# Routing, expert projections and row softmax in one block: routing chunk by chunk, output constants prepared inside

## The reference, cut to what matters

```python
x = x + xattn_ref(layernorm(x), ctx, ctx, ...)      # 32 x 512 x 512, recurrence with gates, 8 heads of 64
h = layernorm(x)                                    # then 16 experts of width 64
def ffn(x, Wg, Wq, bq, Wkv, bkv, Wo, bo, ln_g, ln_b):
    h = transpose(x, (1, 0, 2))                     # 512 tokens, each with 32 candidate rows
    probs = softmax(h @ Wg)                         # over the 16 experts
    idx = sort(top_k(transpose(probs, (0, 2, 1)), cap=2))   # each expert takes 2 of a token's 32 rows
    hg = rows of h at idx
    q = hg @ Wq + bq;  k, v = split(hg @ Wkv + bkv)
    att = (q . k) * 64 ** -0.5                      # 2 x 2 per token and expert
    p = softmax(att, axis=1)                        # over all 512 tokens
    ao = (p @ v) @ Wo + bo
    y = h + scatter_add(ao at idx)
    return transpose(layernorm(y) * ln_g + ln_b)
x = x + ffn(layernorm(x), ...)
```

## Time and profile before

| what | value |
|---|---|
| median of 3 runs | 1986.8 us (1984.19 to 1990.59) |
| the profiled execution | 1991.78 us, span of the core 1990.0 us |
| granted TensorE clock, mean of the span | 0.943 |
| PE busy | 1680.2 us (84%) |
| DVE busy | 1386.0 us (70%) |
| ACT busy | 1087.6 us (55%) |
| POOL busy | 1221.4 us (61%) |

### The profile page before, as it was taken

The page is one execution under the profiler, slowest core; times in us unless marked ns, Lnnn a source line. Parts: engine busy times, 40 slices in busy tenths (PEclk is TensorE's granted clock), DMA queues, the critical chain, the costliest instruction groups (busy, mean ns, idle before and its releaser), DMA issues. The chain is left out here.

```text
span 1990.0 us, 58854 instructions
## 1 busy us (share of the span) xinstructions
PE 1680.2 (84%) x22734; PEld 1281.8 (64%) x22893; DVE 1386.0 (70%) x2931; ACT 1087.6 (55%) x2531; POOL 1221.4 (61%) x1218
## 2 busy tenths in 40 slices
PE   4898888988899888998989861599996799989894
PEld 3677777777777777777777751599995344444442
DVE  2577776777777777777777779233345298999998
ACT  3676776777767777676777640122221545454541
POOL 1566667676676666766767760477673375666664
PEclk9999999999999999999999985699998899999998
DMA  6132222222322222222231010645443257777686
GB/s 198 50 98 86 92 98 82 87 93 97 98 82 87 92 97 98 82 93 89 95 97 61 34 42 0 252 139 139 137 139 101 53 129 170 168 169 171 153 181 154
DMA packets 106597, 218.03 MB, mean 110 GB/s; under 512 B 13008, under 2 KB 14416, under 8 KB 105552
## 3 DMA queue, kind: packets, MB, share of 16 engines
q1 hardware_dynamic: 96080, 180.68, 31.8%
q0 software_dynamic: 10240, 33.56, 5.8%
HBM read 147.08 MB, written 67.11 MB: 108 GB/s over the span
## 5 line engine op out<-in xcount | busy, mean ns | idle before, releaser
L318 POOL TENSOR_TENSOR rec_hn<-rec_hn,rec_out_w 128x512 f32<-128x512 f32 x128 | 199.3, 1557 | 212.9 <-DVE rec_hn L739 212.9
L1320 POOL TENSOR_TENSOR out_x_half<-out_x_half,out_ln_b 128x512 f32<-128x512 f32 x128 | 163.7, 1310 | 154.0 <-DVE out_z_half L1490 154.0
L1424 PE MATMUL out_z_ps<-out_ao,out_hot 32*128 32x512 f32 x2048 | 234.6, 606 | 16.0 <-ACT out_ao L1352 11.5
L296 POOL TENSOR_TENSOR rec_hrs<-rec_harg,rec_minus_half 128x8 f32<-128x8 f32 x128 | 213.0, 1664 | 10.0
L1112 ACT ACTIVATE exp_rows_t<-exp_t_ps 128x512 f32<-128x512 f32 x128 | 69.5, 594 | 244.6 <-PE exp_t_ps L1080 240.0
L1424 PEld LDWEIGHTS out_z_ps<-out_ao,out_hot 32*128 32x128 f32 x2048 | 106.2, 189 | 141.8 <-issue 113.4
L1352 ACT ACTIVATE out_ao<-out_o_ps,sigma_rows 128x512 f32<-128x512 f32 x128 | 88.0, 687 | 193.7 <-PE out_o_ps L1412 193.7
L705 DVE TENSOR_TENSOR rec_c<-rec_s_ps,rec_d 128x512 f32<-128x512 f32 x256 | 164.9, 686 | 38.2 <-PE rec_s_ps L426 35.2
L536 ACT ACTIVATE rec_d<-rec_l_ps 128x512 f32<-128x512 f32 x256 | 151.7, 593 | 62.6 <-PE rec_l_ps L450 61.8
L1092 PE MATMUL exp_q_ps<-exp_wqkv,exp_rows_t 128*128 128x192 f32 x1024 | 178.4, 328 | 0.0
L1092 PEld LDWEIGHTS exp_q_ps<-exp_wqkv,exp_rows_t 128*128 128x128 f32 x1024 | 167.4, 192 | 0.0
(11 more groups left out here) (215 smaller groups left out, 4349.5 us busy)
## 6 DMA issues: line engine op xcount, KB each, us to landing
rec_x_ring<-in_x SPq DMA_DIRECT2D x128, 256.0 KB, 3.0
rec_ctx_ring<-in_ctx SPq DMA_DIRECT2D x128, 256.0 KB, 3.0
x_scratch<-rec_x_ring SPq DMA_DIRECT2D x128, 256.0 KB, 2.0
out_x_half<-x_scratch SPq DMA_DIRECT2D x128, 256.0 KB, 5.5
out<-out_x_half SPq DMA_DIRECT2D x128, 256.0 KB, 3.8
exp_wqkv<-in_wqkv SPq DMA_DIRECT2D x4, 1536.0 KB, 15.3
exp_x_rows<-x_scratch,rowid POOLq DMA_INDIRECT x128
out_wo<-in_wo SPq DMA_DIRECT2D x1, 2048.0 KB, 7.7
```

The lines of the kernel that those rows point to most:

```text
L296: nc.gpsimd.tensor_tensor(hrs[:, G % 2], harg[:, G % 2], mhalf[:], ALU.pow).then_inc(hrs_done, 1)
L318: nc.gpsimd.tensor_tensor(h, h, w8[:], ALU.mult).then_inc(hw_done, 1)
L1320: nc.gpsimd.tensor_tensor(xt[H % XR][:, q, :], xt[H % XR][:, q, :], lb[:], ALU.add).then_inc(xb_done, 1)
L1424: mm = nc.tensor.matmul(z_ps[r][:], hot[B % 2][g, hp, m * P:(m + 1) * P], ao[B % 2][g, hp, :], start=(hp == 0), stop=(hp == HP - 1))
```

## The change

Routing, experts and softmax become one block (`expert_stage`), so three blocks remain.

- The units run chunk outer: `c, h = divmod(m, NE)`. Only chunk 0 is routed before the units; chunk c + 1 is routed by DVE in 14 parts, one behind each unit of chunk c. `rowid_done` holds POOL's gather of a chunk until its indices are there.
- All 16 experts are centred within the first chunk: PE makes the means of experts 0 to 5 before the first unit and one more in each of the units 0 to 9, in two PSUM tiles; ACT copies them to SBUF (`copy_means`), and DVE subtracts the copy.
- The tables for the scatter come between units 46 and 53, by 4 matmuls each in place of 16. DVE sums the products unit by unit.
- The weights of experts 8 to 15 are loaded after the gather of unit 1 has landed; `Wo`, the bias and the vectors are loaded during units 16 to 32. The bias split, `cols` and the one-hot matrix of the first output step (`hot_first`) are made in units 48 to 62.
- In the output block the loads, the split and the first one-hot matrix are gone.

```diff
-def routing_tables(nc, scope, z, keep, tables, gather, consts):
-def expert_attention(nc, scope, z, x1_dram, wqkv, bqkv, tables, gather, vall, att):
-def softmax_over_rows(nc, scope, z, att, tables):
+def expert_stage(nc, scope, z, keep, x1_dram, wqkv, bqkv, wo_in, vecs, consts, tables, gather, prepared, vall, att):
+    UNITS, RING, EARLY = NE * NC, 6, 6
+    @block.sync
+        weights(0)
+        sp.dma_start(iotab[:], consts[26, :, 0:NI]).then_inc(const_in, 16)
+        sp.dma_start(ident[:], consts[0]).then_inc(const_in, 16)
+        sp.dma_start(tokid[:], consts[25]).then_inc(const_in, 16)
+        weights(1)
+        sp.dma_start(bias[:], bqkv).then_inc(b_in, 16)
+        sp.wait_ge(rows_in[1], 32)
+        weights(2)
+        weights(3)
+        sp.wait_ge(transposed, NE)
+        sp.dma_start(bo[:], vecs[0]).then_inc(bo_in, 16)
...
+    @block.gpsimd
+        def fetch(m):
+            c, h = divmod(m, NE)
+            if h == 0:
+                pool.wait_ge(rowid_done, c + 1)
...
+    @block.tensor
+        for h in range(EARLY):
+            weight_means(h)
+        pe.wait_ge(const_in, 48)
+        for m in range(UNITS + 1):
+            if m < UNITS:
+                transposes(m)
+            if m + EARLY < NE:
+                weight_means(m + EARLY)
+            if m == 46:
+                rows_of(m_ps[0], idx).then_inc(ip_full, 1)
+            if m == 50:
+                pe.wait_ge(sel_done, 1)
+                rows_of(m_ps[1], ssel).then_inc(sg_full, 1)
+            if m == 52:
+                pe.wait_ge(ip_read, 1)
...
+            if m > 0:
+                projections(m - 1)
...
+    @block.scalar
+        router_exp(0)
+        for h in range(EARLY):
+            copy_means(h)
+        for m in range(UNITS):
+            evict(m)
+            if m + EARLY < NE:
+                copy_means(m + EARLY)
+            if h == 2 and c + 1 < NC:
+                router_exp(c + 1)
+            if 53 <= m < 61:
+                distance(m - 53)
+            if m in (61, 62):
+                mark(m - 61)
...
+    @block.vector
+        for part_no in range(10):
+            route(0, part_no)
+        centre(0)
+        centre(1)
+        for part_no in range(10, 14):
+            route(0, part_no)
+        dve.wait_ge(b_in, 16)
+        for m in range(UNITS):
+            if m + 2 < NE:
+                centre(m + 2)
+            read(m)
+            if m:
+                logits(m - 1)
+            if c + 1 < NC:
+                route(c + 1, h)
...
+            if m == 50:
+                link(vec.tensor_reduce(colv[:], four[:], AX.X, ALU.add))
+                vec.tensor_scalar(colv[:], colv[:], base, None, ALU.add).then_inc(ip_read, 1)
...
 def output_stage
-        sp.dma_start(bo[:], vecs[0]).then_inc(bo_in, 16)
-        sp.dma_start(wo[:], wo_in).then_inc(w_in, 16)
-        sp.dma_start(lg[:], vecs[1]).then_inc(vec_in, 16)
-        sp.dma_start(lb[:], vecs[2]).then_inc(vec_in, 16)
...
-        pool.wait_ge(vec_in, 32)
-        act.wait_ge(dve_set, 1)
...
         spread(0)
-        for m in range(2):
-            for hp in range(4 * m, 4 * m + 4):
-                distance(0, hp)
-                evict(0, hp)
-            mark(0, m)
+        for hp in range(HP):
+            evict(0, hp)
```

More of the change, by code:

```diff
@@ L1004, in sem @@
         return scope.enter_context(nc.semaphore("exp_" + name))
+    iotab = sb("iotab", [P, NI])
+    peak = sb("peak", [P, NB])
+    total = sb("total", [P, NB])
+    eq = sb("eq", [P, NE, NB])
+    left = sb("left", [P, NE, NB])
+    m1 = sb("m1", [P, NE])
+    first = sb("first", [P, NE])
+    second = sb("second", [P, NE])
+    idx = sb("idx", [P, NC, NE, 2])
+    ssel = sb("sigma_sel", [P, NC, NE, 2])
+    var = sb("variance", [P, NC, NB])
+    each = sb("each_four", [P, 4 * P])
+    four = sb("four", [P, P, 4])
     w = sb("wqkv", [P, NE, KC, W3])
@@ L1094, in projections, with rows_of @@
             mm.then_inc(q_full, 1)
-        weight_means(0)
+        def rows_of(ps, table):
+            flat = table[:].rearrange("p c h i -> p (c h i)")
+            to = ps[:].rearrange("p (c b k) -> p b c k", c=NC, b=4)
+            for b in range(4):
+                mm = nc.tensor.matmul(to[:, b], each[:, P * b:P * b + P], flat, start=(b == 0), stop=(b == 3))
+            return mm
+        for h in range(EARLY):
+            weight_means(h)
+        pe.wait_ge(const_in, 48)
         for m in range(UNITS + 1):
@@ new lines, in _ @@
+            if m == 47:
+                vec.reciprocal(ssel[:].rearrange("p c h i -> p (c h i)"), rsel[:].rearrange("p c h i -> p (c h i)")
+                               ).then_inc(sel_done, 1)
+            if m == 48:
+                vec.tensor_copy(cols[:, 0:P], tokid[:]).then_inc(cols_done, 1)
+                vec.tensor_scalar(cols[:, P:2 * P], tokid[:], float(P), None, ALU.add).then_inc(cols_done, 1)
+                vec.memset(ones[:], 1.0)
+            if m == 49:
+                dve.wait_ge(ip_full, 1)
+                own(m_ps[0])
@@ L1524, in program @@
-        with ExitStack() as routed:
-            keep = (sb(routed, "probs_all", [P, z.NC, NE, NB]), sb(routed, "rstd_all", [P, z.NC, NB]))
-            with ExitStack() as scope:
-                recurrence_stage(nc, scope, NB, (x, ctx, consts, gate_w, gate_b, out_w, wg), x1_dram, keep)
-            with ExitStack() as scope:
-                routing_tables(nc, scope, z, keep, tables, gather, consts)
-        vall = sb(kept, "v_all", [P, z.NC, NE, 2, z.DH])
-        att = sb(kept, "att", [P, z.NC, NE * 4])
@@ L1532, in program, with sb @@
-        with ExitStack() as scope:
-            expert_attention(nc, scope, z, x1_dram, wqkv, bqkv, tables, gather, vall, att)
+        def sb(name, shape, dt=F32):
+            return kept.enter_context(nc.sbuf_tensor(name, shape, dt))
+        probs = sb("probs_all", [P, z.NC, NE, NB])
+        keep = (probs, sb("rstd_all", [P, z.NC, NB]))
+        with ExitStack() as scope:
+            recurrence_stage(nc, scope, NB, (x, ctx, consts, gate_w, gate_b, out_w, wg), x1_dram, keep)
+        tables = tuple(sb(name, [P, P]) for name in ("colv", "sigma_rows", "eps_var", "tokid", "ident2"))
@@ L1536, in program @@
         with ExitStack() as scope:
[L1537 removed]
+            output_stage(nc, scope, z, x1_dram, out, prepared, tables, vall, att)
 def shape_constants():
```

456 lines of the change are left out of this document (205 added, 251 removed).

## The result

| what | before | after |
|---|---|---|
| median of the runs of this comparison | 1988.69 us (1984.19 to 1994.59, 4 runs) | 1908.25 us (1905.3 to 1913.83, 4 runs) |
| span of the profiled execution | 1990.0 us | 1908.6 us |
| granted TensorE clock, mean of the span | 0.943 | 0.965 |
| DVE busy | 1386.0 us | 1406.2 us (74%) |
| POOL busy | 1221.4 us | 1233.8 us (65%) |

The ratio of after to before is 0.9597, with a 95% interval of 0.9561 to 0.9633: 4.0% faster. The forecast was 1907.6 us, counted from a median before of 1986.8; in this comparison the median before is 1988.69. As a gain, 79.2 us were forecast; 80.4 were measured on the medians and 81.4 in the spans.

A forecast was written before the change was run, and what follows sets the result against it. PE bounds the units and the output has DVE and PE busy, but some 145 us are at no engine's limit. Terms 67.8 - 0.4 + 1.9 + 8.0 + 1.9 = 79.2 us take the median from 1986.8 to 1907.6, range 1899 to 1917.

The forecast's parts named there:

- 1. Routing of chunk 0: Start of the new block: DVE's routing ahead of the first gather takes 13.2 us, row numbers at 1202.1 against 1233.
- 2. First gather and first units: From row numbers to first read: first transposes at 1207.1, first read at 1214.8 against 1282.6; gain so far 67.8 us.
- 3. The loop: First to last read of the units: 238.0 us against 237.6, PE work saved is eaten by waits; loss 0.4.
- 4 to 6. Softmax, output start, first evictions: After the last read: shorter way into softmax 1.9, POOL's earlier product 8.0, ACT's marks gone before first scatter 1.9 us gained.
- POOL and DVE in series: Units' loop: descriptor writing too excludes DVE's two-operand work, so their times add; 17 us more, 1925, or 1934; chance 0.17.
- gathers over 1.0: Units' loop: POOL's gathers taking over 1.0 us were listed among the signs that the prediction is wrong.
- Slow opening: Before the first read: gather and third weights share DMA, 6 + 3 lost, PE's clock another 2; 1918; chance 0.12.
- It does not do what it says: Chunk boundaries: DVE five units late with row numbers, each of three boundaries bares a 5 us gather; 1923; chance 0.03.
- PE's clock: Units' loop: waits for DVE keep PE's clock down, 3.6 us more a unit, 2138 with all 64; chance 0.02.

The follow-up runs named there:

- the twins: Changed kernel plus one 512-element DVE operation in every unit, with two SBUF operands or with one: 1916.69 us (ratio 0.9632) and 1909.9 us (0.9597).

## Why the prediction was right

The mechanism held: the routing went beside PE, the opening shrank to one chunk's routing, and the loop kept its length. That the sum came out within 2.2 us of the measured gain is partly luck, since the misses have both signs: 2.0 too much for the opening, 2.9 too little for the loop, 0.9 too much for the evictions, and 1.6 us that the recurrence, with the same code, happened to be shorter.

**1. Routing of chunk 0.** 13.3 us from the block's start to the finished row numbers, against 13.2.

**2. First gather and first units.** The first rows were there 6.0 us behind the finished row numbers; 4.9 was expected. Part of it is the gather's own time: its first instruction took 1.61 in place of 1.18, beside a centring on DVE. The first transposes came at 1206.59, near the 1207.1 of the forecast only since the block had started 1.6 earlier than forecast; from the block's start it was 19.3 against 18.2. From there to the first read it took 8.6 and not 7.7, nearly all of the miss between the projections' start at 1211.61 and the read: 3.6, where I had put PE's 2.7 and nothing for the handover to DVE. Together these terms gave 65.8 of 67.8: 1.1 were lost up to the first transposes and 0.9 behind them.

**3. The loop.** Mis-sized by 2.9 us, and to the good side. The terms for PE's work were right: 231.7 us against 231.2 (218.4, 10.4 and 2.4), with the reads 3.48 apart. The waits were 3.5 us against 6.8: 1.5 for `ip_read` against 1.8; two at the start, 1.3 for weights and the 0.5 that lie inside the loop of the 1.4 for rows, against the single 3; and 0.0 for DVE's reads, where 2 us stood for DVE and POOL excluding each other. This last is the largest miss of the sum.

**4 to 6. Softmax, output start, first evictions.** The way into the softmax gave 2.0 of 1.9. POOL's chain took 8.1 us from the block's start to the first attention values, against the 8.2 of the forecast. The evictions gained 1.0 instead of 1.9: PE's clock was low for three projections, and not for two as in the kernel before, so the fourth began 5.85 us behind the first and not 4.92. The term had priced ACT's marks and not what PE would run at. Part of this miss is noise, since in a further execution of the change the third projection took 1.10 in place of 1.53. Why the clock rises where it does stays open; a shorter start alone is not the reason, since with the zeros on VectorE the start was shorter still and already the second projection took 1.09.

**The rivals.** *POOL and DVE in series* was right in its mechanism and wrong in its price. The gathers are slowed. Groups by line, first the kernel before, then the kernel after:

```profile
L1043 POOL DMA_INDIRECT exp_x_rows<-x_scratch,rowid x128 | 124.1, 969 | 30.2 <-issue 22.4
```
```profile
L954 POOL DMA_INDIRECT exp_x_rows<-x_scratch,rowid x128 | 136.5, 1066 | 45.5 <-issue 25.0 <-DVE rowid L1152 16.0 <-DVE att L1184 0.3
```

Before, the slowest took 1.18 us; after, 1.73 (at 1217.90, 0.05 behind the start of a centring of 0.96). The sum over 128 is 12.4 us, where the rival's full addition would have been 17 or more on PE. POOL runs several units ahead of PE, so what a gather loses is taken from that lead. With a mean of 1.07 us the prediction's own sign of being wrong, "gathers over 1.0", did come, and the time did not follow it: the sign was badly chosen. The Trainium skill, SBUF — State Buffer, "Who interferes with whom", infers that descriptor writing is spared beside a VectorE operation with two SBUF inputs. The trace disagrees for a gather: the first instruction of the block took 1.61 beside the centring of 1200.52, against 1.18 alone at 1259.92; later ones took up to 1.73 against 0.95; and the twins' means are 1100 against 1028 ns. Whether it is the writing of descriptors that is held or the gather's reading of its row numbers, no run separates. The prediction said that the first rival would hold if that inference were wrong. It is wrong here, and the rival did not hold: that step of the argument failed. My term rested on rows 11, and both my 2 us and the rival's 17 were too much. In rows 11 I had also misread what was left of DVE's operation when POOL's began: 0.52 us (0.68 less 0.16), of which POOL's lost 0.40.

*Slow opening* did not come (19.3 us from the block's start to the transposes), but the experiment on the last weights shows that it was real: without SP's wait it costs 7.2 us at the first read, of which the loop gives back 3.6. *It does not do what it says*: POOL waited for row numbers three more times after the opening, 2.6 us in all and 1.0 at the longest, and PE never for that. *PE's clock*: 1.00 in the loop.

## What to carry to other kernels

Work that stands alone on one engine costs its whole length; the same work cut to pieces shorter than the slack of each unit costs almost nothing, even where it slows its neighbours, as long as the column "idle before" of the bounding engine shows none of it. So price a mutual delay by whose lead it eats, not by the busy time it adds. And behind a gap, ask at what clock PE's first operations run: savings that end in the same clock rise do not add, and the moment of the clock's rise moves a start like this one by about one microsecond from run to run.

## What was not expected of the hardware

- An indirect gather's instruction on POOL slows when DVE work with two SBUF operands is under way as it starts (0.95 alone, up to 1.73 us beside).
- DVE's two-operand operation slows beside POOL's work too: 1.12 in place of 0.68 us where POOL's product had started 0.17 before it. Beside a gather alone the trace is divided: the operation at 1298.80, begun inside a gather, took 1.24, the one at 1204.42, begun inside another, 0.69.
- The gather of 256 KB lands later beside bulk loads: with 3 MB more in flight the first rows came 4.7 us later.
- PE's idle times of 1.8 and 2.4 us ahead of the first transposes left them at the high level (1.07 and 1.06); idle times of 3.3 and 6.5 us did not (1.65 and 1.94); all had means at the high level before them. Inside the loop 1.5 us at unit 52 left the projections behind it at 2.87, while 2.2 and 2.7 us made them 4.55.
- The same four loads at the start of the output block landed after 10 us in one kernel and after 13 in another. This stays open.
